# Second attention: the bias is added on VectorE, and each head's exponential is taken before the transpose

## The reference, cut to what matters

```
q = einsum('bfd,dnh->bfnh', layernorm(x), wq) * 8 ** -0.5
k = einsum('btd,dnh->btnh', ctx, wk);   v = einsum('btd,dnh->btnh', ctx, wv)
logits = einsum('btnh,bfnh->bnft', k, q) + bias          # bias: 128 x 128 per batch, the same for all heads
x = x + einsum('bfnh,nhd->bfd', einsum('bnft,btnh->bfnh', softmax(logits), v), wo)
```

## Time and profile before

| | us |
|---|---|
| median of 3 runs (lowest, highest) | 1594.14 (1593.96, 1597.61) |
| the profiled execution's own time | 1592.65 |
| its span, first to last instruction | 1590.9 |
| busy, matmuls on TensorE | 1520.8 |
| busy, VectorE | 1363.6 |
| busy, ScalarE | 1178.6 |
| busy, GpSimd | 968.3 |

### The profile page before, as it was taken

One profiled execution on the slowest core, in us unless ns is written; L12 is line 12 of the kernel. 1 busy time (PEld: TensorE's weight loads), 2 busy tenths in 40 slices (PEclk: granted clock), 3 DMA queues, 4 the chain that ended last, 5 costly groups with the idle time before them and its releaser, 6 DMA issues.

```text
span 1590.9 us, 34527 instructions
## 1 busy us (share of the span) xinstructions
PE 1520.8 (96%) x10399; PEld 1061.7 (67%) x10555; DVE 1363.6 (86%) x4496; ACT 1178.6 (74%) x3951; POOL 968.3 (61%) x1432
## 2 busy tenths in 40 slices
PE   4778999999999999999999999999999999999997
PEld 2456766776776677777667767767776776677654
DVE  3777888898888889888888988888988888898986
ACT  3555777777777778777787877778777777777776
POOL 3223667667666666766666666666676657666557
PEclk9679999999999999999999999999999999999999
DMA  4520000000000000000000000000000000000000
GB/s 124 141 57 18 18 20 19 10 12 19 20 19 20 19 8 13 20 19 19 20 19 9 13 20 19 19 20 18 10 13 20 20 19 20 15 10 8 11 2 4
DMA packets 87137, 36.07 MB, mean 23 GB/s; under 512 B 29672, under 2 KB 86952, under 8 KB 86952
## 3 DMA queue, kind: packets, MB, share of 16 engines
q1 hardware_dynamic: 70312, 25.48, 7.2%
q10 hardware_dynamic: 16640, 8.39, 1.9%
HBM read 19.16 MB, written 2.10 MB: 13 GB/s over the span
## 4 chain that ended last, share of the span: by engine, by line
PE 87%; POOL 4%; issue 3%; DVE 3%; DMA 2%; ACT 1%; SPq 1%; POOLq 0%; ACTq 0%; DVEq 0%
PE psC L293 51%; PE psA L293 15%; PE psB L293 12%; PE psB L521 4%; PE psC L617 2%; PE psB L541 1%; POOL accO L1768 1%; POOL TE L1756 1%; PE psA L411 1%; PE psA L454 1%; SPq L1839 1%; POOL v_sb L1761 1%; DVE TE L1474 1%; DMA raw<-in_L_ffn_o_w 1%; DMA raw<-in_L_ffn_v_w 1%
## 5 line engine op out<-in xcount | busy, mean ns | idle before, releaser
L769 ACT ACTIVATE TE<-psC,gateO 128x128 f32<-128x128 f32 x1024 | 294.4, 383 | 58.6 <-POOL accO L1768 49.4
L769 ACT ACTIVATE TE<-psC,gate 128x128 f32<-128x128 f32 x1024 | 294.9, 387 | 41.1 <-PE psC L293 38.6
L1474 DVE SCALAR_TENSOR_TENSOR TE<-psC,gateO,TE 128x128 f32<-128x128 f32 x1024 | 286.5, 343 | 38.9 <-ACT TE L769 27.6
L1474 DVE SCALAR_TENSOR_TENSOR TE<-psC,gate,TE 128x128 f32<-128x128 f32 x1024 | 287.5, 343 | 21.9 <-PE psC L293 13.4
L293 PE MATMUL psC<-Oh,ch 128*128 128x512 f32 x512 | 267.5, 522 | 0.9 <-DVE TE L1474 0.8
L293 PE MATMUL psC<-Vh,xTh 128*128 128x512 f32 x512 | 264.6, 517 | 1.9 <-DVE TE L1474 1.1
L1768 POOL TENSOR_TENSOR accO<-accO,TE 128x512 f32<-128x512 f32 x192 | 247.3, 1288 | 13.5 <-DVE TE L1474 3.9
L1756 POOL TENSOR_TENSOR TE<-TE 128x256 f32<-128x256 f32 x256 | 188.5, 736 | 52.9 <-DVE TE L1474 51.6
L293 PE MATMUL psC<-Vh,xTl 128*128 128x512 f32 x512 | 202.2, 395 | 0.0
L1720 POOL TENSOR_SCALAR_AFFINE_SELECT PTA<-PTA 128x512 f32<-128x512 f32 x128 | 82.3, 646 | 196.1 <-ACT PTA L769 193.6
L293 PE MATMUL psC<-Oh,cl 128*128 128x512 f32 x512 | 201.1, 393 | 0.0
(11 more groups left out here) (234 smaller groups left out, 3856.5 us busy)
## 6 DMA issues: line engine op xcount, KB each, us to landing
bdB<-Ks SPq DMA_DIRECT2D x128, 64.0 KB, 2.0
bdA<-QKb SPq DMA_DIRECT2D x128, 32.0 KB, 1.9
raw<-in_L_ffn_v_w ACTq DMA_DIRECT2D x8, 512.0 KB, 4.2
raw<-in_L_ffn_o_w ACTq DMA_DIRECT2D x8, 512.0 KB, 4.3
x_sb<-in_x SPq DMA_DIRECT2D x32, 64.0 KB, 1.9
ctx_sb<-in_ctx SPq DMA_DIRECT2D x32, 64.0 KB, 2.0
mrow_i<-in_mask_BxS_if SPq DMA_DIRECT2D x32, 64.0 KB, 3.2
bias_sb<-in_mask_Bx1xSxS_ff SPq DMA_DIRECT2D x32, 64.0 KB, 2.0
```

The source lines that it names most:

```text
L769: return A.activation(o, i, func, **kw)
L1474: m = V.scalar_tensor_tensor(TE[:, i, e], psC[:, p, e * P:(e + 1) * P], gates[:, e:e + 1], TE[:, i, e], ALU.mult, ALU.add)
```

## The change

On TensorE the two bias matmuls of each group go; a single matmul gives the scores. bh, bl and the two steps that made them go as well. On VectorE a step `b_bias` takes psB and the bias, broadcast over the four heads, adds them and writes PTB; `b_max` then reads PTB in SBUF, and `b_less` is gone. On ScalarE `b_exp` takes the exponential of each head by itself, in place in PTB, with the negated maximum as the per-partition bias; after the transposes a new step `b_trans` copies psB back to PTB. The transposes now wait for the exponentials, and the first two groups' also for the addition of group t + 2, which still has scores in the same bank. `b_pvs` and `b_ut` wait for the copies.

All five `period` functions are written in a new order. The periods are renumbered by one (a_ steps i - 1, b_ steps i - 2, and so on), so that the distance in periods between the stages of a batch is what it was, and each list starts at another point of the cycle.

```
 b_scores (TensorE)
-                    pe.wait_ge(b_bl, b + 1)
                     pe.wait_ge(b_qs, b + 1)
...
-                    pe.wait_ge(b_e, 4 * b + t - 1)
-                o = heads_of(psB[:, t % 2, :])
-                mm(o, ident_r[:], over_heads(bh[:], NJ), True, False)
-                mm(o, ident_r[:], over_heads(bl[:], NJ), False, False)
+                    pe.wait_ge(b_b, 4 * b + t - 1)
                 pe.wait_ge(s_bdB, 64 * (b + 1))
-                mm(o, Qs1[:, t, :], bdB[:, t], False, True).then_inc(b_s, 1)
+                mm(heads_of(psB[:, t % 2, :]), Qs1[:, t, :], bdB[:, t]).then_inc(b_s, 1)
 b_trans (TensorE)
-                pe.wait_ge(b_d, 4 * b + t + 1)
+                pe.wait_ge(b_e, 4 * b + t + 1)
+                if t < 2:
+                    pe.wait_ge(b_b, 4 * b + t + 3)
+                else:
+                    pe.wait_ge(b_c, 4 * b + t - 1)
 b_pvs (TensorE)
-                    pe.wait_ge(b_e, 4 * b + max(t, 2) + 1)
+                    pe.wait_ge(b_c, 4 * b + max(t, 2) + 1)
 ScalarE
-            def b_bias(b):
-                copy(bh[:], bias_sb[:, b % 2]).then_inc(b_bh, 1)
...
             def b_exp(b, t):
+                act.wait_ge(b_nm, 4 * b + t + 1)
+                for j in range(NJ):
+                    m = copy(PTB[:, t, j], PTB[:, t, j], ACT.Exp, bias=nmB[:, t, j:j + 1])
+                m.then_inc(b_e, 1)
+            def b_trans(b, t):
                 act.wait_ge(b_t, 4 * b + t + 1)
-                copy(flat(PTB[:, t]), psB[:, t % 2, :], ACT.Exp).then_inc(b_e, 1)
+                copy(flat(PTB[:, t]), psB[:, t % 2, :]).then_inc(b_c, 1)
 VectorE
+            def b_bias(b, t):
+                dve.wait_ge(b_s, 4 * b + t + 1)
+                dve.wait_ge(s_bias[b % 2], 16 * (b // 2 + 1))
+                dve.wait_ge(b_pv, b)
+                V.tensor_tensor(PTB[:, t], heads_of(psB[:, t % 2, :]), over_heads(bias_sb[:, b % 2], NJ),
+                                ALU.add).then_inc(b_b, 1)
             def b_max(b, t):
-                dve.wait_ge(b_s, 4 * b + t + 1)
-                V.tensor_reduce(nmB[:, t, :], heads_of(psB[:, t % 2, :]), AX_X, ALU.max, negate=True).then_inc(b_nm, 1)
-            def b_less(b, t):
-                V.tensor_tensor(PTB[:, t], heads_of(psB[:, t % 2, :]), along(nmB[:, t, :], P), ALU.add).then_inc(b_d, 1)
+                dve.wait_ge(b_b, 4 * b + t + 1)
+                V.tensor_reduce(nmB[:, t, :], PTB[:, t], AX_X, ALU.max, negate=True).then_inc(b_nm, 1)
 GpSimd
-            def b_bias(b):
-                G.tensor_tensor(bl[:], bias_sb[:, b % 2], f(bh[:]), ALU.subtract).then_inc(b_bl, 1)
```

More of the change, by code:

```diff
@@ new lines, in period @@
+                values(i - 4, 0, 0)
+                values(i - 4, 1, 1)
+                b_trans(i - 2, 2)
+                a_scores2(i - 1, 2)
+                a_scores2(i - 1, 3)
+                c_scores(i - 3, 0)
+                b_trans(i - 2, 3)
+                c_scores(i - 3, 1)
+                values(i - 4, 1, 0)
+                b_pvs(i - 2)
+                a_pvs(i - 1)
+                values(i - 4, 2, 1)
+                b_ut(i - 2)
+                a_ut(i - 1)
+                values(i - 4, 2, 0)
@@ new lines, in period @@
+                values(i - 4, 3, 1)
+                a_att(i - 1)
+                values(i - 4, 3, 0)
+                values(i - 4, 4, 1)
+                b_att(i - 2)
+                a_proj(i - 1)
+                values(i - 4, 4, 0)
+                values(i - 4, 5, 1)
+                values(i - 4, 5, 0)
+                values(i - 4, 6, 1)
+                values(i - 4, 6, 0)
+                b_keys(i - 1)
+                values(i - 4, 7, 1)
+                a_x1t(i - 1)
+                values(i - 4, 7, 0)
@@ new lines, in period @@
+                a_route(i - 1)
+                c_context(i - 4)
+                a_shared(i - 1)
+                b_proj(i - 2)
+                outputs(i - 4, 0, 1)
+                outputs(i - 4, 0, 0)
+                a_ht(i - 1)
+                outputs(i - 4, 1, 1)
+                outputs(i - 4, 1, 0)
+                a_ffn(i - 1)
+                outputs(i - 4, 2, 1)
+                a_ctxt(i)
+                outputs(i - 4, 2, 0)
+                a_xt(i)
+                a_keys(i)
+                outputs(i - 4, 3, 1)
@@ L1047, in period @@
             def period(i):
+                b_trans(i - 2, 3)
+                c_exp(i - 3, 0)
                 if i == 2:
+                    cut(10)
+                b_unnorm(i - 2)
+                if i == 1:
+                    cut(1)
+                a_unnorm(i - 1)
+                c_exp(i - 3, 1)
+                values(i - 4, 2)
+                if i == 1:
+                    cut(2)
+                if i == 2:
+                    cut(11)
+                a_att(i - 1)
+                values(i - 4, 3)
@@ new lines, in period @@
+                a_proj(i - 1)
+                b_att(i - 2)
+                values(i - 4, 4)
+                values(i - 4, 5)
+                values(i - 4, 6)
+                if i == 1:
+                    cut(3)
+                if i == 2:
+                    cut(12)
+                b_keys(i - 1)
+                a_x1t(i - 1)
+                values(i - 4, 7)
+                c_context(i - 4, 0)
+                if i == 1:
+                    cut(4)
+                if i == 2:
+                    cut(13)
@@ new lines, in period @@
+                a_gap(i - 1)
+                c_short(i - 4, 0)
+                a_shared(i - 1, 0)
+                c_context(i - 4, 1)
+                c_short(i - 4, 1)
+                a_shared(i - 1, 1)
+                outputs(i - 4, 0)
+                if i == 1:
+                    cut(5)
+                if i == 2:
+                    cut(14)
+                a_ht(i - 1)
+                outputs(i - 4, 1)
+                if i == 1:
+                    cut(6)
+                a_ctxt(i)
@@ new lines, in period @@
+                if i == 0:
+                    weights1()
+                if i == 2:
+                    cut(15)
+                a_xt(i)
+                outputs(i - 4, 2)
+                a_queries(i)
+                a_keys(i)
+                b_xt(i - 1)
+                outputs(i - 4, 3)
+                outputs(i - 4, 4)
+                if i == 1:
+                    cut(7)
+                b_queries(i - 1)
+                outputs(i - 4, 5)
+                outputs(i - 4, 6)
+                if i == 1:
+                    cut(8)
@@ new lines, in period @@
+                b_values(i - 1)
+                a_values(i)
+                c_trans(i - 3, 0)
+                outputs(i - 4, 7)
+                if i == 1:
+                    cut(9)
+                a_values2(i)
+                b_exp(i - 1, 0)
+                c_trans(i - 3, 1)
+                c_xt(i - 2)
+                b_exp(i - 1, 1)
+                values(i - 3, 0)
+                c_gexp(i - 2)
+                b_trans(i - 1, 0)
+                b_exp(i - 1, 2)
+                c_products(i - 2, 0)
@@ new lines, in period @@
+                a_stats(i - 1, 1)
+                c_share(i - 4, 2)
+                c_context(i - 5, 0)
+                if i == 2:
+                    cut(4)
+                if i == 3:
+                    cut(13)
+                a_routed(i - 2, 0)
+                c_weights(i - 5, 1)
+                a_routed(i - 2, 1)
+                a_stats(i - 1, 2)
+                a_routed(i - 2, 2)
+                c_share(i - 4, 3)
+                c_weights(i - 4, 0)
+                c_context(i - 5, 1)
@@ new lines, in period @@
+                outputs(i - 5, 5)
+                b_bias(i - 2, 0)
+                outputs(i - 5, 6)
+                b_max(i - 2, 0)
+                if i == 2:
+                    cut(8)
+                b_bias(i - 2, 1)
+                if i == 1:
+                    selectors()
+                a_max(i - 1, 0)
+                b_max(i - 2, 1)
+                a_max(i - 1, 1)
+                b_bias(i - 2, 2)
+                a_max(i - 1, 2)
+                a_max(i - 1, 3)
+                a_maxt(i - 1, 0)
@@ new lines, in period @@
+                a_maxt(i - 1, 1)
+                c_xl_(i - 3)
+                b_max(i - 2, 2)
+                a_withmax(i - 1)
+                b_bias(i - 2, 3)
+                outputs(i - 5, 7)
+                c_choice(i - 3, 0)
+                c_choice(i - 3, 1)
+                b_max(i - 2, 3)
+                c_choice(i - 3, 2)
+                c_products(i - 3, 0)
+                c_products(i - 3, 1)
+                values(i - 4, 0)
+                c_choice(i - 3, 3)
+                c_max(i - 3, 0)
@@ L1618, in _ @@
+                a_stats2(i - 1, 1)
+                a_stats2(i - 1, 2)
+                values(i - 4, 5)
             zeros()
@@ new lines, in period @@
+                a_causal(i - 1, 0)
+                a_causal(i - 1, 1)
+                result(i - 5, 0)
+                result(i - 5, 1)
+                a_causal(i - 1, 2)
```

(35 more changed lines are left out.)

455 lines of the change are left out of this document (128 added, 327 removed).

## The result

| us | before | after |
|---|---|---|
| median of 4 runs (lowest, highest) | 1594.05 (1592.98, 1597.61) | 1574.80 (1573.38, 1576.64) |
| the profiled execution's own time | 1592.65 | 1576.64 |
| its span | 1590.9 | 1574.9 |

The ratio is 0.9876, with a 95% interval of 0.9857 to 0.9895. The change makes the kernel faster by 1.2%, 19.3 us. The time lies in the range of the third case (half eaten, 1563 to 1588), but not for the reason given there.

What follows compares the result with a forecast made beforehand. TensorE was taken to bound the kernel; 29 steady intervals x 1.4 us = 40.6, plus 1 us for the first two, gave 1592.65 - 41.6 = 1551.0 us, range 1534 to 1592.

Steps and rivals of the forecast that it cites:

- the third case: Half eaten: VectorE keeps 1.4 us of gaps waiting for ScalarE's longer queue; 1574 us (1563 to 1588), chance 0.18.
- The bound before: TensorE sets the time before the change: matmul row busy 96% of the span, 46.23 of 46.56 us a batch.
- TensorE's saving: Eight bias matmuls a batch go from the second attention's scores, 0.237 us each: 1.87 us a batch.
- VectorE: Addition replaces subtraction at equal cost, maximum from SBUF unchanged: zero, bounds -0.4 and +0.1 us a batch.
- The rule weighed there: SBUF access takes VectorE 62 cycles less than PSUM: 65 ns per maximum, 0.26 us a batch; not adopted.
- ScalarE's price: Sixteen exponentials by head at 0.29 us, less a bias copy: net +4.4 us a batch, 35.9 to 40.3.
- The wait for accO: ScalarE's 1.71 us wait for a TE slot before output 7 would go, by the new GpSimd order.
- What the batch can become: Dense stretch (second attention's query scaling to division): ScalarE's excess slides out, VectorE keeps 0.5 us gaps; 1.4 us saved.
- Rival 5: ScalarE ends the dense stretch, from 0.38 us per exponential: slower, 1617 us (1598 to 1630), chance 0.15.
- Rival 3: VectorE's static order waits for ScalarE's longer queue, leaving 0.6 us a batch; 1574 us (1563 to 1588), chance 0.18.
- The signs named for a wrong mechanism: A batch shorter than 44.7 us, or TensorE waiting for PTB or psB over 1.5 us a batch.
- The first two batches: The opening, two intervals of 37.6 us: 1 us gain for both, bounds 0 and 8.6.

Runs made afterwards that it cites:

- e2: The changed kernel with one exponential of 128x512 per group in place of four of 128x128; 1546.82 us.
- e12: e2 with two copies of 128x1024 per batch added to ScalarE outside the dense stretch; 1547.70 us.
- e9: e7 with the second attention's maximum taken over only the first 64 keys of each head; 1543.14 us.
- e6: The changed kernel with the second attention's maximum taken over only the first 64 keys of each head; 1574.74 us.
- e3: The changed kernel with ScalarE's copy of the last group moved ahead of the four scalings of expert 1; 1574.61 us.
- e8: The kernel before with each 128x512 exponential taken as four of 128x128 with a per-partition operand, out of PSUM; 1627.55 us.
- e4: The changed kernel with the maximum subtracted on GpSimd, one 128x512 exponential per group out of PSUM on ScalarE, and e3's order; 1577.14 us.
- e7: e4 with one call moved: GpSimd's sum of output 6 comes behind the third subtraction; 1555.86 us.

## Why the prediction was wrong

Point by point, by its own steps.

**The bound before**: right. TensorE ended the batch. Three kernels of the new order come down to the same 44.95 to 44.97 us, with ScalarE light in the dense stretch (e2, e12) or with ScalarE and VectorE both relieved (e9), and TensorE's matmuls are busy 44.95, 44.95 and 44.68 us of it.

**TensorE's saving**: 1.87 us forecast for all eight passes (8 x 0.2375 would have been 1.90), 46.56 - 44.96 = 1.60 the most that a run of the new order gave. Against that the term was 0.27 too large, about 8 us; why no run shows more stays open. What the new order alone is worth was not run either. The sum was also taken from the profiled execution; from the median, 1.5 us above it, it would have given 1552.5.

**VectorE**: the addition was to take 687 ns and takes 681 to 684; the maximum was to stay at 687 and takes 677. The range was kept. The rule weighed there, from the Trainium skill, "VectorE: DVE Perf Modes", section on the TRN2 errata (62 cycles less from SBUF), is not borne out: 10 ns and not 65. VectorE's sum a batch was put at 41.5 and is 42.1, for the most part because two steps of the expert choice with both operands in SBUF last longer, as these groups after show (600 to 1060 us; before, their means were 466 and 281 ns; the last section has what they meet on GpSimd):

```profile
L1407 DVE TENSOR_TENSOR gt<-gp,best 128x128 f32<-128x128 f32 x20 | 14.3, 713 | 0.3
L1409 DVE TENSOR_TENSOR gt<-gt,earlier 128x128 f32<-128x128 f32 x20 | 8.3, 417 | 0.3
```

**ScalarE's price**: the durations were right to the hundredth, 0.29 us an exponential and 40.3 us a batch. The wait for accO went, from 49.4 us in the whole span to:

```profile
ACT TE L768 <- POOL accO L1766: 1.8, 3, 0.8
```

**The step that failed** is "What the batch can become". I saw that ScalarE would be 1.4 us over in the dense stretch and wrote that its later steps "slide into the loose stretch, which has 5.8 us for it", at no cost, and then took VectorE's gaps, 0.5 us, as what is left. The runs show the other way round. A lighter VectorE gains nothing (e6), and ScalarE's excess is paid: 0.85 us a batch (e2), 25 us of the kernel. The loose stretch did have the room (e12 put 40.28 - 38.44 = 1.84 us there for nothing), but by the waits in the kernel what would have had to slide could not do so free of charge: b_pvs waits for the last copy, b_ut for b_unnorm behind it, and the experts' psC banks for c_exp behind that, all in one list on ScalarE, and TensorE runs that order too. e3 shows it in small. In the terms of my sum, 1.87 - 0.47 = 1.40, the measured ones are 1.60 - 0.85 = 0.75. That it meets the 0.74 is no check, for both terms are measured from the same batch of about 44.96 us.

**The rivals.** Rival 5 named the mechanism, ScalarE ending the dense stretch, and was wrong on when it bites: I let it start at 0.38 us an exponential, as if a queue cost nothing until it is full and then all. It already cost 0.85 us at 0.29. Rival 3 had the size by VectorE waiting for ScalarE, and e6 speaks against that as well. The signs named for a wrong mechanism were weak: TensorE's waits for PTB in the steady batches are under 1.5 us, 0.35 us a batch on matmuls and 1.05 on weight loads, and such waits are only a part of what the late queue costs.

**The first two batches**: I gave 1 us of gain. The traces show a loss. The fifth copy Vb, from which on the batches are steady, before and after (tile Vb, 172 to 200 us):

```profile
L769 ACT ACTIVATE Vb<-psA x1: 278/278/278, 182.0 to 182.0; 128x128 bf16<-128x128 f32 x1
L768 ACT ACTIVATE Vb<-psA x1: 278/278/278, 186.9 to 186.9; 128x128 bf16<-128x128 f32 x1
```

The opening takes 4.9 us longer after the change. The same copy starts at 185.4 us in e3 and 185.7 in e6, which have the changed kernel's exponentials too, and at 182.7 in e2, so most of this loss seems to go with the exponentials as well. From there to the last copy Vb (1439.2 before, 1423.9 after) 20.2 us are gained, and 0.7 behind it: 20.2 - 4.9 + 0.7 = 16.0 us, the difference of the two spans. The medians differ by 19.3, as the profiled execution after is the slowest of its four.

## What to carry to other kernels

With one order per engine, cost new work by its place: list what the same engine must still do before the next thing that the bounding engine waits for, and charge new work there even where the engine shows gaps. In this kernel it cost a third to a half of its length (0.38 in e2, 0.5 in the old order in e8). Idle time elsewhere in the cycle helps only if those steps can be moved there. And to learn which engine ends a stretch, make one of its steps there cheaper and then another engine's: the two runs e2 and e6 told more than all busy shares.

## What the runs showed of the hardware

GpSimd can shut VectorE out for a whole instruction. In e4 a 0.20 us cast within SBUF lasted 1.19 us, until GpSimd's sum had ended, and cost about 0.77 us in every batch (46.00 against 45.23 in e7). The Trainium skill, "SBUF — State Buffer", section "Who interferes with whom", says that a VectorE cast can run in a mode that takes the pair of ports shared with GpSimd, that whoever issues first then has the pair for the whole instruction, and that a VectorE operation with two SBUF inputs contends with a GpSimd instruction that reads SBUF. The trace agrees, with 740.55 and 740.61 us as the two ends. In the changed kernel gt<-gp,best, with two SBUF inputs, has its mean at 713 ns against 466 before. The one at 746.39 lasts 0.55 us and ends at 746.94, GpSimd's sum beside it at 746.79; the one at 752.73 lasts 0.87 and ends at 753.60, GpSimd's sum at 753.45. VectorE's additions and full maxima with at most one input in SBUF kept means of 675 to 689 ns in every kernel, with GpSimd's four new subtractions too. ScalarE's short exponentials from SBUF with a per-partition operand follow each other at 0.29 us, against 0.25 out of PSUM in e8 (four hand over after 1.00 us).
